# W_out with its mean taken out on the chip, squares summed on ScalarE, one VectorE operation for scale and add: a linear-attention and expert kernel on Trainium2

## The reference

```python
def _layernorm(x, axis=-1, eps=1e-05):
    m = jnp.mean(x, axis=axis, keepdims=True)
    v = jnp.var(x, axis=axis, keepdims=True)
    return (x - m) / jnp.sqrt(v + eps)
...
    # attention, per head:  q_phi, k_phi = random features of the rotated q, k
    S = jnp.einsum('chlm,chld->chmd', k_phi, v)
    sum_k = jnp.sum(k_phi, axis=2)
    numer = jnp.einsum('chlm,chmd->chld', q_phi, S)
    denom = jnp.maximum(jnp.einsum('chlm,chm->chl', q_phi, sum_k), EPS)
    out_heads = numer / denom[..., None]
    out = out_heads.transpose(0, 2, 1, 3).reshape(C, L, E)
    return out @ w_out.T
...
    x = x + _layernorm(_L0_attn_ref(_layernorm(x, axis=-1), ...), axis=-1)
    x = x + _layernorm(_L0_ffn_ref(_layernorm(x, axis=-1), ...), axis=-1)
```

## Time and profile before

| | us |
|---|---|
| median of 3 runs (2091.22 to 2094.61) | 2093.01 |
| the profiled execution's own time | 2092.85 |
| its span, first to last instruction | 2091.1 |
| busy in the span: PE, DVE, ACT, POOL | 1820.3, 1206.9, 1121.7, 775.4 |
| first and last scatter of slots begin at | 955.62, 1412.68 |

### The profile page before, as it was taken

One profiled execution on the slowest core, in us unless ns is written; L12 is line 12 of the kernel. 1 busy time (PEld: TensorE's weight loads), 2 busy tenths in 40 slices (PEclk: granted clock), 3 DMA queues, 4 the chain that ended last, 5 costly groups with the idle time before them and its releaser, 6 DMA issues.

```text
span 2091.1 us, 33695 instructions
## 1 busy us (share of the span) xinstructions
PE 1820.3 (87%) x12931; PEld 891.9 (43%) x12976; DVE 1206.9 (58%) x2230; ACT 1121.7 (54%) x1371; POOL 775.4 (37%) x718
## 2 busy tenths in 40 slices
PE   8999999999969998798889887446999989997785
PEld 6444444444447885132333333223444444443332
DVE  7776767676620000367898898851443434345886
ACT  5565555555436665586778776413443444442443
POOL 0000000000000000025888788874777777761110
PEclk9999999999989999999999998777999999999897
DMA  7444444446368885777787665342899999988984
GB/s 250 163 141 179 141 179 142 178 139 211 107 172 209 213 211 132 174 206 180 244 253 220 211 221 191 130 172 73 201 202 228 242 238 236 204 146 247 332 289 144
DMA packets 188848, 405.15 MB, mean 194 GB/s; under 512 B 33812, under 2 KB 72084, under 8 KB 172064
## 3 DMA queue, kind: packets, MB, share of 16 engines
q1 hardware_dynamic: 83184, 222.41, 35.7%
q10 hardware_dynamic: 68640, 124.26, 16.9%
q0 software_dynamic: 36864, 56.32, 14.4%
HBM read 237.06 MB, written 177.08 MB: 198 GB/s over the span
## 4 chain that ended last, share of the span: by engine, by line
DVE 15%; POOL 12%; issue 11%; PE 11%; DMA 9%; ACT 3%; SPq 0%; POOLq 0%; DVEq 0%; ACTq 0%
POOL slot_dram L1262 6%; DMA acc_dram<-s_y,s_slot 5%; POOL acc_dram L1428 3%; PE s_gates L1487 3%; PE s_ups L1487 2%; PE s_ys L1502 2%; DVE s_heads L1103 1%; DMA s_rows<-rows_dram,s_slot 1%; DVE s_stats L1653 1%; DVE s_x L1672 1%; POOL s_rows L1414 1%; ACT s_xT L1533 1%; PE s_y L900 1%; PE s_turned L1464 1%; POOL s_rstd L1255 1%
## 5 line engine op out<-in xcount | busy, mean ns | idle before, releaser
L1262 POOL DMA_INDIRECT slot_dram<-keep_filled,keep_slots x256 | 313.1, 1223 | 86.5 <-issue 73.0
L261 PE MATMUL s_proj<-s_xT,keep_wqkv 128*128 128x512 f16 x1536 | 341.8, 379 | 0.3 <-DVE s_by_sin L391 0.3
L1428 POOL DMA_INDIRECT acc_dram<-s_y,s_slot x128 | 202.2, 1580 | 101.0 <-issue 36.4
L900 PE MATMUL s_y<-keep_wo,s_at_hl 128*128 128x512 f16 x768 | 192.8, 405 | 44.0 <-ACT s_z L990 44.0
L261 PEld LDWEIGHTS s_proj<-s_xT,keep_wqkv 128*128 128x128 f16 x1536 | 147.7, 98 | 183.7 <-issue 12.6
L1542 ACT ACTIVATE s_gate<-s_gates 128x512 f32<-128x512 f32 x96 | 57.1, 597 | 263.5 <-PE s_ups L1487 218.0
L1612 DVE SCALAR_TENSOR_TENSOR s_h<-s_gate,s_ups 128x512 f32<-128x512 f32 x96 | 65.9, 686 | 216.4 <-ACT s_gate L1542 216.4
L341 POOL TENSOR_SCALAR s_rstd<-s_mv 128x4 f32<-128x4 f32 x16 | 16.0, 998 | 462.3 <-DVE s_mv L356 462.3
L678 ACT ACTIVATE s_phi<-s_logits 128x1024 f32<-128x1024 f32 x128 | 130.9, 1023 | 85.0 <-PE s_logits L699 85.0
L520 ACT ACTIVATE s_hl<-s_rot 128x1024 f16<-128x1024 f32 x64 | 67.6, 1056 | 200.0 <-DVE s_rot L402 193.1
L238 PE MATMUL s_proj<-keep_wqkv,s_xT 128*128 128x512 f16 x768 | 172.5, 381 | 0.0
(11 more groups left out here) (165 smaller groups left out, 3196.9 us busy)
## 6 DMA issues: line engine op xcount, KB each, us to landing
s_x<-x_in SPq DMA_DIRECT2D x32, 1024.0 KB, 9.3
qk_dram<-s_hl ACTq DMA_DIRECT2D x32, 1024.0 KB, 6.7
keep_ahead<-qk_dram SPq DMA_DIRECT2D x48, 512.0 KB
acc_dram<-s_zero SPq DMA_DIRECT2D x17, 1024.0 KB, 13.4
v_dram<-s_v ACTq DMA_DIRECT2D x16, 1056.0 KB, 5.6
s_v<-v_dram SPq DMA_DIRECT2D x16, 1056.0 KB, 11.0
s_spread<-share_dram SPq DMA_DIRECT2D x64, 256.0 KB
x_dram<-s_x ACTq DMA_DIRECT2D x16, 1024.0 KB, 5.5
```

The costliest lines, as they stand in the source:

```text
L261: mm = nc.tensor.matmul(out[:, 512 * b:512 * b + 512], left, right, start=(c == 0 and i == 0), stop=(c == EC - 1 and i == 2))
L900: mm = nc.tensor.matmul(y[m % 2][:], at_hl[n % 2][:, s, c, a * P:(a + 1) * P], keep["wo"][:, w, c, :], start=(c == 0 and i == 0), stop=(c ...
L1262: nc.gpsimd.indirect_dma_start(out=io["slot"], out_offset=bass.IndirectOffsetOnAxis(ap=slots[n % 2][:, a * K + j:a * K + j + 1], axis=0), ...
L1428: nc.gpsimd.indirect_dma_start(out=io["acc"], out_offset=bass.IndirectOffsetOnAxis(ap=slot[e % RING][:, a, 0:1], axis=0), in_=y[e % 2][:, ...
```

## The change

In the first stage VectorE takes the mean over the output features out of every row of the transposed W_out (`centre_wo`, between groups 1 and 2), so every row of the projected tile has mean zero and its variance is its mean square. ScalarE then squares the projected tile with a sum along the row (`square`), in place of `make_z`; `measure_y` and its aggregate go; and `add` computes tile x rstd + x in one operation with the projected tile read from PSUM. All lags behind that shrink by one, and `add` runs ahead of `make_low`.

```diff
+            def centre_wo():
+                dve.wait_ge(w_out_loaded, 16)
+                for c in range(EC):
+                    ins = nc.vector.bn_stats(wo_stats[:, c, :], w_out[:, c, :])
+                ins.then_inc(wo_measured, 1)
+                dve.wait_ge(wo_measured, 1)
+                for c in range(EC):
+                    ins = nc.vector.bn_aggr(wo_mean[:, c, :], wo_stats[:, c, :])
+                ins.then_inc(wo_averaged, 1)
+                dve.wait_ge(wo_averaged, 1)
+                for c in range(EC):
+                    ins = nc.vector.tensor_scalar(w_out[:, c, :], w_out[:, c, :], wo_mean[:, c, 0:1], None, ALU.subtract)
+                ins.then_inc(wo_centred, 1)
...
+                if n == 1 and j == 3:
+                    centre_wo()
...
             def make_wo_high():
-                act.wait_ge(w_out_loaded, 16)
+                act.wait_ge(wo_centred, 1)
...
-        PROJECT, MEASURE, SCALE, ADD, SPLIT, TURN, COPY, GATE = 8, 9, 10, 11, 12, 13, 14, 14
-        SCORE, CHOOSE, PLACE, WEIGH, FILL, SEND = 18, 18, 19, 19, 21, 21
+        PROJECT, SQUARE, ADD, SPLIT, TURN, COPY, GATE = 8, 9, 10, 11, 12, 13, 13
+        SCORE, CHOOSE, PLACE, WEIGH, FILL, SEND = 17, 17, 18, 18, 20, 20
...
                 if m >= 2:
-                    pe.wait_ge(z_ready, m - 1)
+                    pe.wait_ge(x1_ready, m - 1)
...
-            def make_z(m):
+            def square(m):
                 k = m % 2
+                act.wait_ge(y_ready, m + 1)
+                if m >= 2:
+                    act.wait_ge(var_ready, m - 1)
+                nc.scalar.activation(squares[k][:], y[k][:], ACT.Square, scale=E ** -0.5,
+                                     accum_out=mv[k][:, 0, 1:2]).then_inc(y_squared, 1)
...
-            def measure_y(m):
-                dve.wait_ge(y_ready, m + 1)
-                nc.vector.bn_stats(stats[m % 2][:, 0, :], y[m % 2][:]).then_inc(y_measured, 1)
...
             def add(m):
-                dve.wait_ge(z_ready, m + 1)
+                dve.wait_ge(rstd_ready, m + 1)
...
-                nc.vector.tensor_tensor(x[n % XS][:, a, :], x[n % XS][:, a, :], z[m % 2][:], ALU.add).then_inc(x1_ready, 1)
+                at = x[n % XS][:, a, :]
+                nc.vector.scalar_tensor_tensor(out=at, in0=y[k][:], scalar=rstd[k][:, 0:1], in1=at, op0=ALU.mult,
+                                               op1=ALU.add).then_inc(x1_ready, 1)
...
+                if 0 <= s - ADD < NT:
+                    add(s - ADD)
                 if 0 <= s - TURN < NT:
                     make_low(s - TURN)
                 if 0 <= s - ADD < NT:
-                    add(s - ADD)
-                if 0 <= s - MEASURE < NT:
-                    measure_y(s - MEASURE)
-                if 0 <= s - ADD < NT:
                     measure_x1(s - ADD)
-                if 0 <= s - MEASURE < UNITS:
-                    aggregate(s - MEASURE)
+                    aggregate(s - ADD)
...
             def make_rstd(u):
                 k = u % 2
-                pool.wait_ge(mv_ready, u + 1)
+                if u < NT:
+                    pool.wait_ge(y_squared, u + 1)
+                if u >= 1:
+                    pool.wait_ge(mv_ready, u)
```

More of the change, by code:

```diff
@@ L151, in setup_and_project_stage @@
                                "feat_high", "feat_low", "w_high", "w_low", "wo_high"))
+        wo_measured, wo_averaged, wo_centred = (t.sem(n) for n in ("wo_measured", "wo_averaged", "wo_centred"))
         block = ctx.enter_context(nc.Block())
@@ L776, in attend_and_route_programs @@
         x = [t.sb(f"x{r}", [P, A, E]) for r in range(XS)]
-        z, xn = t.pair("z", [P, E]), t.pair("xn", [P, E])
+        squares, xn = t.pair("squares", [P, E]), t.pair("xn", [P, E])
         hl = t.pair("hl", [P, A, 2, E], F16)
         xT = t.pair("xT", [P, 2, EC, G], F16)
-        stats = t.pair("stats", [P, 2, 6])
-        mv, rstd, shift = t.pair("mv", [P, 2, 2]), t.pair("rstd", [P, 2]), t.pair("shift", [P, 2])
+        stats = t.pair("stats", [P, 6])
+        mv, rstd, shift = t.pair("mv", [P, 2, 2]), t.pair("rstd", [P, 2]), t.pair("shift", [P, 1])
         power, eps = t.sb("power", [P, 2]), t.sb("eps", [P, 2])
@@ L1043, in act_program @@
                     make_phi(s + 1, 0)
-                if 0 <= s - SCALE < NT:
-                    make_z(s - SCALE)
+                if 0 <= s - SQUARE < NT:
+                    square(s - SQUARE)
                 if s < NT:
@@ L1108, in make_at_low, with make_shift @@
                                         ALU.subtract).then_inc(at_low_ready, 1)
[L1110 to L1117, removed]
+            def make_shift(m):
+                k = (m + 1) % 2
+                dve.wait_ge(rstd_ready, m + 2)
+                if m >= 2:
+                    dve.wait_ge(xn_ready, m - 1)
+                nc.vector.scalar_tensor_tensor(out=shift[k][:], in0=mv[k][:, 1, 0:1], scalar=-1.0, in1=rstd[k][:, 1:2],
@@ L1135, in aggregate @@
-            def aggregate(u):
-                k = u % 2
-                if u < NT:
-                    dve.wait_ge(y_measured, u + 1)
-                    ins = nc.vector.bn_aggr(mv[k][:, 0, :], stats[k][:, 0, :])
-                if u >= ADD - MEASURE:
-                    dve.wait_ge(x1_measured, u - (ADD - MEASURE) + 1)
-                    ins = nc.vector.bn_aggr(mv[k][:, 1, :], stats[k][:, 1, :])
-                ins.then_inc(mv_ready, 1)
+                nc.vector.bn_stats(stats[m % 2][:], x[m // A % XS][:, m % A, :]).then_inc(x1_measured, 1)
@@ L1145, in make_low, with aggregate @@
+            def aggregate(m):
+                dve.wait_ge(x1_measured, m + 1)
+                nc.vector.bn_aggr(mv[(m + 1) % 2][:, 1, :], stats[m % 2][:]).then_inc(mv_ready, 1)
             def make_low(m):
@@ L1209, in dve_program @@
                     read_total(n)
-                if 0 <= s - SCALE < UNITS:
-                    make_shift(s - SCALE)
+                if 0 <= s - SPLIT < NT:
+                    make_shift(s - SPLIT)
                 n = group_at(s, PLACE + 1)
```

37 lines of the change are left out of this document (16 added, 21 removed).

## The result

The changed kernel takes 2105.25 us against 2094.12 (medians of ten runs each): ratio 1.0051, interval 1.0036 to 1.0066. Forecast were 2076 and a gain; it is slower by half a per cent. The profiled execution took 2103.91 with a span of 2102.1, 11.0 more than before.

The account below looks back on a forecast made before the run. GpSimd was taken to pace attention and routing. From 2092.85 us: +4.5 centring, -7 earlier start, -16 fewer held sends, +2 late fills = -16.5, so 2076 us; 8 in 10 range 2063 to 2090.

Parts of the forecast that it names:

- The bound: Attention and routing stage: GpSimd sets the pace, from the first send at 955.62 to the last at 1412.68 us.
- Held sends: Attention and routing: with add ahead of make_low, GpSimd's sends escape being slowed by make_low; 16 us saved, bounds 0 and 20.
- Start: Pipeline one step shorter in attention and routing: first send 7 us earlier, bounds 4 and 9.
- Centring: First stage, VectorE between tile groups 1 and 2: no slack, so all 4.5 us are lost, bounds 3.8 and 5.3.
- Square at nothing: ScalarE, attention and routing: Square replacing make_z takes 0.59 us to twice 0.78; effect on the time zero.
- Fill behind the share: VectorE, attention and routing: fill now stands behind a wait for a transfer; costs 2 us in all, bounds 0 and 15.
- The margin: GpSimd's send is due 9.4 us after VectorE reads the denominator, fill ends at 9.0: 0.4 us to spare.
- B: Attention and routing: slots become the pace, fill misses its send by 1.6 us in 15 groups; 2098 us, chance 0.12.
- A: Attention and routing: slowed sends only move to other operations, or make_low slows none; 2092 us, chance 0.18.
- C: Attention and routing: make_low's 20 us and some of divide, at_low go, first send 9 earlier; 2066 us, chance 0.08.
- What follows the last send: From the last send to the end: length stays 678 us, if the early shared passes stay hidden.

Follow-up runs that it names:

- the run with fill ahead: Changed kernel with fill moved ahead of make_share in VectorE's order; ratio 0.997 to the kernel before, 2080.53 us.
- the third q buffer: Changed kernel with a third buffer for q, so that its load is issued behind the load of x; ratio 0.9937 to the kernel before.

## Why the prediction was wrong, point by point

**The bound.** That GpSimd paces the stage of attention and routing fits the kernel before: an earlier place for q's load gained nothing there (0.9995). In the changed one GpSimd waits for VectorE, and VectorE for a transfer.

**Held sends, -16.** Right: -13.9. Against VectorE's timeline, 45 sends began under make_low and lost 18 us before; 22 do after and lose 5.6. The 25 that begin under the new add alone lose 0.06 us each (1083.26, under the add of 1083.17, took 1.03; the next, under the statistics behind make_low, 0.97). Read as a rule for these sends, the aside of the Trainium skill, "SBUF — State Buffer", section "Who interferes with whom", has no tensor_tensor hold one; the 22 under make_low still lose 0.26 us on average, so the measurement decides against it here too.

**Start, -7.** Nearly: the first send is 0.2 us later, and the first stage ends 598.44 - 592.49 = 5.9 later, so the shorter pipeline gave 5.7; counted from the first denominator (839.51, then 844.21) it gave 4.5.

**Centring, +4.5.** Right in the mechanism, 5.9 in this execution, above the bound of 5.3. The windows view, 109 to 151 us:

```profile
109.00:151.00 42.00, 36.51 (x196) 16.58 (x191) 29.80 (x43) 21.60 (x25) 4.29 (x4) 0.96 0.38 132
```

The granted clock is 0.96 of full here. In the run with fill ahead, which has the same first stage, it was 1.00 in that stretch, and the group cost 40.8 - 36.3 = 4.5 us more than before, against 42.1 - 36.3 = 5.8 here. So 1.3 us go with the lower clock. The waits are the same in both executions, so they alone don't explain it.

**Square at nothing.** Right in size: 593 + 204 = 0.80 us, in two instructions, against 0.78 for the old operation.

**Fill behind the share, +2 (0 to 15).** This is the step that failed. The waits for the slots within the stretch of sends grew from 8.6 - 3.1 = 5.5 to 50.4 - 6.9 = 43.5, by 38; the sends gave 13.9 back, and the rest, 8.8 us, is other idle time that went; that leaves the 15.3. It failed in two ways. The margin of 0.4 us was worked out with the transfer's duration of before, 5.2 us, as if that were a property of the transfer. It is one of its neighbours: 4.7 to 5.6 with q behind it; 7.2 to 16.2 in eight groups running of the changed kernel, with q 9 to 12 us ahead; 7.8 to 16.3 in the first thirteen groups of the old kernel with q later. And nothing in the prediction asked what else the queue issues just before. The margin itself was also a little too large: where the way is 5.4 us, with the third q buffer, sends still wait some 1 us. So the term was too small even without q: with the third buffer the waits within the stretch are 37.0 - 4.1 = 32.9, still 27 above those before and outside the bound of 15.

The distance of q alone doesn't set the length. The third and fourth group of the kernel before have q 8.0 and 9.2 us ahead and take 5.5 and 6.0; there no store of x stands between q and the denominators, as it does in the changed kernel's groups of 6.9 us and more from the fourth on. The first group has no such store either, q 5.4 us ahead, and takes 7.8. So nearness counts; whether x's store adds to it is not shown. And the sixth group is long with q at any distance ahead: 13.6 in the kernel before, 18.0 with the third buffer; only q behind the share made it short (5.3).

The Trainium skill, "DMA: Bandwidth & Descriptors", section "Queues, rings and completion order", says that SP has one ring on each DMA engine, consumed in order. By that, loads of q queued on SP stand in front of the denominators by rule; the traces agree (storing the denominators 5.7 us with q 9.1 us ahead, 2.4 with q issued behind the share).

**Why q came nearer.** The load of q waits for TensorE's logits; these came later against VectorE, since the exps stand behind the score, which waits for fill (64.8 us). That fits the trace, and freeing the score moved q from mostly 9.9 to mostly 12 to 14 us ahead, but the time gained is inside the intervals; with fill ahead the score waits only 13.9 us, and q still stands 9.9 to 17 us ahead. How much of the approach is due to the score and how much to the shorter pipeline stays open.

**Rivals.** B was the case: its mechanism and its place, at a chance of 0.12 and with 2098 too low, since the way grew by 2.0 to 6.5 us in nine of the sixteen groups and the sends waited 2.3 to 12.7 us for fill in eight groups. A and C did not occur. With q out of the way and the centring in pieces, the rest of the sum came out at two thirds of the forecast: 16.5 + 4.5 = 21 us expected, ratio 0.9929, about 15 us (10 to 19), measured, with 25.3 us of waits for the slots left.

**What follows the last send** was to keep its length; it is 4.5 us shorter (678.4 to 673.9), and why stays open.

## What to carry to other kernels

A transfer's duration read from a trace belongs to what is queued around it; before a step is moved behind its landing, list what each queue issues ahead of it, and ask which of it the change brings nearer. When one engine gets room, the next bound may be, as here, a round trip through memory that nobody had waited for; keep other work between its start and its use (here fill), and give its neighbours an earlier place (a third buffer). Small jobs on a chain without slack go in pieces into the waits that the trace shows, not whole in front of the next link.

## What the runs showed that was not expected

A change of one semaphore's number, q's load one tile of logits later, cost the old kernel 1.9%, nearly four times what the change itself lost. A Square with an accumulated sum costs 0.20 us more than the copy of such a tile. And TensorE, after waits of 1.4, 0.9 and 3.3 us in one tile group, was granted 0.96 of its full clock (its upper level, 2.4 GHz) over that group in one execution, and all of it in two others with the same waits.
